# Audio tower on one core: setup moved into the first stage, shift products moved between projection halves, first groups of the last stage shared by VectorE and POOL

## What is computed

```python
# 1: attentive pooling of windows of 4 positions, stride 2 -> 127 patches
A = tanh(x @ W_w.T + W_b + b);  scores = A @ V_w.T + V_b
w = softmax(scores[:, idx]);    h = (w * x[:, idx]).sum(-2) @ P_w.T + P_b
# 2: attention of 8 heads in three parts on a normalized h
h = h + attn(layernorm(h)) @ w_proj.T + b_proj
# 3: four experts, the best one by the router's logits
n = layernorm(h);  e = argmax(n @ router_w + router_b)
h = h + (gelu(n @ w1[e] + b1[e]) @ w2[e] + b2[e] + n)
```

## Time and profile before

| | us |
|---|---|
| median of 3 runs | 1978.07 |
| the profiled execution | 1976.59 |
| its span | 1974.8 |
| setup block | 0 to 30.3 |
| tokenize | 30.6 to 404 |
| attend | 409 to 1492 |
| feed_forward | 1497 to 1975 |
| PE / DVE / ACT / POOL busy | 1814 / 1488 / 1477 / 1263 |

### The profile page before, as it was taken

The page is one execution under the profiler, slowest core; times in us unless marked ns, Lnnn a source line. Parts: engine busy times, 40 slices in busy tenths (PEclk is TensorE's granted clock), DMA queues, the critical chain, the costliest instruction groups (busy, mean ns, idle before and its releaser), DMA issues. The chain is left out here.

```text
span 1974.8 us, 58866 instructions
## 1 busy us (share of the span) xinstructions
PE 1814.1 (92%) x20032; PEld 1012.3 (51%) x20032; DVE 1487.6 (75%) x3655; ACT 1476.9 (75%) x2983; POOL 1262.7 (64%) x2323
## 2 busy tenths in 40 slices
PE   1898889859999999999999999999993999999998
PEld 0566556624444444444444444444442666666666
DVE  3666666768999999999999999999973555555554
ACT  1666666528899999999889989999983666666665
POOL 2666666546777777777777777777744565656551
PEclk9999999969999999999999999999996999999999
DMA  5433433224444444444444444444431222323232
GB/s 142 107 85 90 101 85 99 50 36 81 87 90 88 90 88 88 90 89 89 88 88 89 90 88 90 88 89 88 88 70 27 64 68 63 69 61 69 61 72 49
DMA packets 504063, 159.64 MB, mean 81 GB/s; under 512 B 452176, under 2 KB 503248, under 8 KB 504016
## 3 DMA queue, kind: packets, MB, share of 16 engines
q1 hardware_dynamic: 504016, 159.04, 37.9%
HBM read 37.41 MB, written 12.48 MB: 25 GB/s over the span
## 5 line engine op out<-in xcount | busy, mean ns | idle before, releaser
L726 DVE TENSOR_REDUCE tops<-p_maxa 128x6 f32<-128x762 f32 x512 | 483.1, 944 | 65.1 <-PE p_maxa L568 62.0
L639 PE MATMUL p_o<-probs,vn 127*32 127x256 f32 x6144 | 411.6, 386 | 0.2 <-DVE att L754 0.2
L564 PE MATMUL p_s<-qm,kt 32*128 32x256 f16 x3072 | 401.8, 276 | 2.0 <-DMA qm<-qk 1.0
L680 ACT ACTIVATE probs<-p_s 128x512 f32<-128x512 f32 x512 | 305.6, 597 | 109.1 <-PE p_s L564 95.6
L728 DVE TENSOR_REDUCE tops<-p_maxb 128x4 f32<-128x508 f32 x512 | 346.6, 677 | 0.0
L1000 DVE TENSOR_TENSOR gel_lo<-gel,gel_hi 128x512 f16<-128x512 f32 x192 | 147.1, 766 | 217.4 <-ACT gel_hi L990 216.0
L686 ACT ACTIVATE probs<-p_s 128x512 f32<-128x512 f32 x512 | 308.6, 603 | 0.0
L683 ACT ACTIVATE probs<-p_s 128x512 f32<-128x512 f32 x512 | 304.3, 594 | 0.3 <-PE p_s L564 0.2
L568 PE MATMUL p_maxa<-kt,qt 24*128 24x256 f16 (+1 forms) x2048 | 283.4, 250 | 15.1 <-DMA kt<-qk 8.6
L777 POOL TENSOR_TENSOR qk<-raw,one 128x384 f16<-128x384 f32 x128 | 105.8, 827 | 221.6 <-ACT raw L702 221.6
L982 ACT ACTIVATE gel<-f_w,b 128x512 f32<-128x512 f32 x192 | 131.9, 687 | 144.0 <-PE f_w L933 144.0
(11 more groups left out here) (209 smaller groups left out, 4544.0 us busy)
## 6 DMA issues: line engine op xcount, KB each, us to landing
xt_a<-in_xt SPq DMA_DIRECT2D x32, 512.0 KB, 4.4
xt_b<-in_xt SPq DMA_DIRECT2D x64, 256.0 KB, 5.2
out<-out_sb SPq DMA_DIRECT2D x32, 336.0 KB, 2.7
xt<-hx SPq DMA_TRANSPOSE x128, 2.3
kt<-qk SPq DMA_TRANSPOSE x128, 2.7
qt<-qk SPq DMA_TRANSPOSE x128, 2.5
qm<-qk SPq DMA_TRANSPOSE x128, 2.7
yt<-ay SPq DMA_TRANSPOSE x128, 2.3
```

Of the source, the lines that this page charges most:

```text
L564: return nc.tensor.matmul(o, kt[full(j), r, kind, g, :], qm[full(j), r % 2, versions, g, :], start=True, stop=True, skip_group_check=True)
L639: last = nc.tensor.matmul(p_o[32 * j:32 * j + 32, blocks, :], vn[0:NP, r, src:src + 32], probs[0:NP, r % 2, QUAD * g + j, kind * 256:(kind ...
L680: nc.scalar.activation(probs[:, r % 2, h + 1, 0:512], p_s[1][:, :, :].rearrange("p x n -> p (x n)"), ACT.Exp, scale=SCALE).then_inc(act_e1 ...
L726: nc.vector.tensor_reduce(top[:, q, pair, 4:10], p_ma[:, 0:6, 0:NP], AX.X, ALU.max, negate=True).then_inc(dve_ma[u], 1)
```

## The change

- The setup block is gone. Its loads, VectorE's splits and POOL's matrices are in tokenize. SyncE issues four loads for the first stage's matrices, then the first input, `vw` and `vb`, the second input, and only then the 17 other weights. VectorE makes the first stage's matrices before its loop; the other weights are split in ten portions (`later_weights`), one after each of blocks 2 to 11. TensorE waits for the matrices instead of for a constant.
- In tokenize a projection is made in two halves. The down-shift is between the halves of step 1, the up-shift between those of step 3. VectorE runs softmax step 0 and 1 at steps 1 and 2, behind the band and ahead of the score; step 2 is at step 3, ahead of the band.
- In attend the waits for constants stand at the first use: TensorE's at i = -2, ScalarE's and POOL's at i = -3.
- In feed_forward VectorE makes the high and low halves of the first two groups (`halves`), POOL the rest of them; the fill of `pk` is in three parts and POOL waits only for the part that it needs; SyncE issues the transpose of an input ahead of that of the packed part while i < 0.

The core of the diff:

```diff
@@ tokenize, SyncE @@
+            for dst, src in ((wtf[0][:, :], dram["wt"][0:128, :]), (wtf[1][:, :], dram["wt"][128:256, :]),
+                             (btf[CB:128, :], dram["bt"][CB:128, :]), (tokf[CB:128, :], dram["tok"][CB:128, :])):
+                sp.dma_start(dst, src).then_inc(tok_loaded, 16)
+            load_xt(0, 0)
+            for dst, src in ((t.vw[:, :], dram["vw"]), (t.vb[:, :], dram["vb"])):
+                sp.dma_start(dst, src).then_inc(row_loaded, 16)
+            load_xt(1, 1)
+            for name, parts in splits:
+                for k, w in enumerate(parts):
+                    sp.dma_start(w[:, :], dram[name][128 * k:128 * (k + 1), :]).then_inc(loaded, 16)
...
@@ tokenize, TensorE @@
-            pe.wait_ge(ones, 2)
+            pe.wait_ge(tok_made, 4)
+            pe.wait_ge(built, 3)
...
+                        project(par, k, 0)
-                    if k == 0 and within(i - 1, NG):
+                    if k == 1 and within(i - 1, NG):
 
                         pe.wait_ge(dve_score, seen(i * G))
                         nc.tensor.matmul(p_down, t.below[:, :], score[:, 1 - par, :, 0:2],
                                          start=True, stop=True).then_inc(pe_down, 1)
-                    if k == 2 and within(i - 1, NG):
+                    if k == 3 and within(i - 1, NG):
 
                         pe.wait_ge(dve_weight, seen(i))
                         nc.tensor.matmul(p_up, t.above[:, :], weight[:, 1 - par, :, 2:4],
                                          start=True, stop=True).then_inc(pe_up, 1)
+                    if within(n, NB):
+                        project(par, k, 1).then_inc(pe_a, 1)
...
@@ tokenize, VectorE @@
+                        if k == G - 1:
+                            softmax(i, 1 - par, 2)
                         dve.wait_ge(pool_diag, seen(u + 1))
...
                         last.then_inc(dve_band, 1)
+                    if k in (1, 2):
+                        softmax(i, 1 - par, k - 1)
                     if within(n, NB):
                         dve.wait_ge(act_tanh, seen(n + 1))
...
-                    softmax(i, 1 - par, k)
...
+                    if isinstance(i, int) and 2 <= n < 12:
+                        later_weights(n - 2)
@@ feed_forward, VectorE @@
-            nc.vector.memset(pk[:, :, :, :].rearrange("p r g n -> p (r g n)"), 0.0).then_inc(consts, 1)
+            nc.vector.memset(one[:, :], 1.0)
+            nc.vector.memset(flat(0, 1), 0.0).then_inc(consts, 1)
+            nc.vector.memset(flat(1, 2), 0.0).then_inc(consts, 1)
+
+            def halves(i):
+
+                for k in range(G):
+                    n = (i + 2) * G + k
+                    x = hx[:, i % 2, k, :]
+                    dve.wait_ge(act_ln, n + 1)
+                    nc.vector.tensor_copy(x[:, 0:C], hn[:, k % 2, :]).then_inc(dve_x, 1)
+                    dve.wait_ge(dve_x, 2 * n + 1)
+                    nc.vector.tensor_tensor(x[:, C:2 * C], hn[:, k % 2, :], x[:, 0:C], ALU.subtract).then_inc(dve_x, 1)
+
+            halves(-2)
+            nc.vector.memset(flat(2, U), 0.0).then_inc(consts, 1)
+            halves(-1)
+            dve.wait_ge(consts, 3)
```

More of the change, by code:

```diff
@@ L358, in _, with diagonal @@
         def _(pool):
+            n = 0
+            def diagonal(m, base, value=1.0):
+                nonlocal n
+                nc.gpsimd.memset(m[:, :], 0.0).then_inc(zeroed, 1)
+                n += 1
+                pool.wait_ge(zeroed, n)
+                nc.gpsimd.affine_select(out=m[:, :], in_=m[:, :], compare_op=ALU.not_equal, fill=value, base=base,
+                                        pattern=[[-1, 128]], channel_multiplier=1).then_inc(built, 1)
+            diagonal(t.ident, 0)
+            diagonal(t.below, -1)
+            diagonal(t.above, 1)
+            far = t.split["w1"][3][CB:128, :]
+            pool.wait_ge(built, 3)
+            nc.gpsimd.memset(far, FAR).then_inc(zeroed, 1)
+            n += 1
+            pool.wait_ge(zeroed, n)
+            nc.gpsimd.affine_select(out=far, in_=far, compare_op=ALU.is_ge, fill=0.0, base=0,
+                                    pattern=[[1, NE * HID]], channel_multiplier=-HID).then_inc(zeroed, 1)
+            n += 1
+            pool.wait_ge(zeroed, n)
+            nc.gpsimd.affine_select(out=far, in_=far, compare_op=ALU.is_ge, fill=0.0, base=HID - 1,
+                                    pattern=[[-1, NE * HID]], channel_multiplier=HID).then_inc(built, 1)
+            pool.wait_ge(built, 4)
+            for e in range(NE):
+                nc.gpsimd.memset(t.rank[:, :, e:e + 1], float(NE - e))
             def body(i, par, half):
@@ L550, in _ @@
         def _(pe):
-            pe.wait_ge(consts, 3)
             full = lambda j: slice(32 * j, 32 * j + 32)
@@ L874, in ready, with turn_x @@
                 sp.sem_inc(sp_ready, 1)
+            def turn_x(i, r):
+                if within(i + 2, NG):
+                    ready(pool_x, seen((i + 3) * G))
+                    if isinstance(i, int) and i < 0:
+                        ready(dve_x, (i + 3) * 2 * G)
+                    if isinstance(i, int) and i == -1:
+                        ready(dma_x, 16)
+                    if within(i - 2, NG):
+                        ready(pe_w[HCH - 1], seen(i - 1))
+                    sp.dma_start_transpose(xt[:, (r + 2) % U].rearrange("p g k n -> p (g k) n"),
+                                           hx[:, r % 2].rearrange("p g n -> p (g n)")).then_inc(dma_x, 16)
             def body(i, r, half):
+                if isinstance(i, int) and i < 0:
+                    turn_x(i, r)
                 if within(i - 1, NG):
@@ L1056, in body @@
                     return
+                first = isinstance(i, int) and i < 0
+                if isinstance(i, int) and i <= 0:
+                    pool.wait_ge(consts, i + 3)
                 for k in range(G):
```

205 lines of the change are left out of this document (90 added, 115 removed).

## The result

| | us |
|---|---|
| before, median of 4 | 1978.14 (1976.28 to 1980.55) |
| after, median of 4 | 1944.74 (1944.09 to 1946.12) |
| ratio | 0.9833, 95% interval 0.9821 to 0.9846 |
| span of the profiled execution | 1974.8 before, 1942.9 after |

The change gains 33.4 us by the medians and 31.9 by the two spans. The forecast was 1941, with 1930 to 1947 as the range of its own case and 1928 and 1972 as low and high end. The time lies in both; how the sum came about is another matter, and the larger part of what follows.

A forecast was written before the change was run, and what follows sets the result against it. The first stage was taken as bound by its setup prelude, then a ring through all engines (11.29 us a cycle). Gains 23.7 + 6.7 + .6 + 4.8 = 35.8 off 1976.59 gave 1941; low end 1928, high end 1972.

The forecast's parts named there:

- (a): Setup moved into the first stage: first projection matmul at 13.0 instead of 40.56, 27.5 us less.
- (b): Later weights split over ten blocks of the first stage: 3.8 us lost, bounds 1.5 and 8.
- (c): Shift products between projection halves in the first stage: cycle 11.05 instead of 11.29, 6.7 us gained over 28 cycles.
- (d): Waits for constants moved in the attention stage: .6 us gained, bounds 0 and .7.
- (e): First groups of the last stage, halves shared with VectorE: 4.8 us gained, bounds 2.5 and 7.5.
- The port is lost: First stage: POOL's next lo beats `weight` to the shared port, cycle 12.15, 31 us more, 1972 in all; chance .16.
- the race: First stage: `weight` against POOL's next lo for the shared port, forecast to be won with .06 us in hand.
- slower: First stage: TensorE's clock falls after the pause, .16 more per matmul; nothing gained, or 1995 with twelve; chance .03.
- TensorE bound: First stage: cycle falls to 9.7, TensorE's work alone, 38 us more gained, 1903 in all; chance .08.
- the ring: First stage: a chain of dependences through all engines sets the cycle, 11.29 us before and 11.05 after.

The follow-up runs named there:

- late_casts: Changed kernel with the later weights' casts and subtractions in the last ten blocks of the first stage's last three groups, not blocks 2 to 11: 1945.65 us.
- spread: Changed kernel with negated maximum in PSUM, softmax ahead of the band at steps 1 and 2, later weights' casts one to a block from block 7: 1900.30 us.
- psum_least: Changed kernel with the negated maximum of the scores in PSUM instead of SBUF: 1940.52 us, ratio .9815 to the kernel before.
- pool_halves: Changed kernel with POOL again making the halves of the last stage's first two groups, the shorter clearing kept: 1949.87 us, ratio .9869 to the kernel before.
- undo_last: Changed kernel with the last stage of the kernel before: 1954.60 us, ratio .9888 to the kernel before.
- h_first: Changed kernel with ScalarE's copy h of step 1 ahead of the exponential instead of behind it: 2005.60 us, ratio 1.0151 to the kernel before.
- ahead: Changed kernel with the softmax at steps 1 and 2 ahead of the band on VectorE: 1904.18 us, ratio .9623 to the kernel before.

## Why the prediction was right, and where it was not

By its own steps:

(a) *First matmul.* Forecast 13.0, measured 13.55: 27.0 gained instead of 27.5. ScalarE starts at 10.33 instead of 9.9, the matmul 3.22 behind it instead of 3.07. The method (issues, landing, the way through the engines) held.

(b) *The later weights.* The term that was mis-sized: 3.8 forecast, 7.2 measured (27.0 at the first matmul, 19.8 left by the fifth down-shift: 92.66 before, 74.36 after, and 1.46 for its later place in the cycle), inside its bounds of 1.5 and 8. The last load was forecast near 24 and is there at 23.43; VectorE stands 2.00, not 3.4. What was left out are three things. The third input is queued on SyncE behind those loads (3.69 on ScalarE). TensorE's clock falls to .50 for 3.4 us at 26.9, behind its wait of 1.89 for a score at the first down-shift; it is busy throughout, so this costs up to 1.7, an estimate from half the busy time. And later instructions meet POOL at the port, on either side: the first cast takes 1.25 behind a lo, the last difference, of one row, 1.21, and POOL's diag 1.61 behind the largest difference:

```profile
48.68 1.42 DVE L273 TENSOR_TENSOR w_lo<-w2f,w_hi 128x1152 f16<-128x1152 f32 x1
...
48.96 1.61 POOL L381 TENSOR_TENSOR diag<-ident,weight 128x256 f32<-128x256 f32 x1
```

late_casts shows VectorE's work to be what holds these groups, the clock's fall included (5.2 back by the fourth down-shift); spread shows the input right behind it.

(c) *The cycle.* Forecast 11.05 by a ring that ends at the up-shift with a wait of 1.3; measured 11.13, with a wait of 1.37 at ph of step 2 and none at the up-shift. The number was nearly right and the path wrong. Up to `shifted` every step is as forecast (lo of step 1 first at the port by .15, `shifted` 1.03 for .97). The step that failed is the next: in working out the lost port I listed ScalarE's queue behind the exponential, h among it, and never asked who waits for h. TensorE does, at ph of step 2, 1.5 ahead of the up-shift. That the wait found there, 1.37, is as long as the one forecast, 1.3, is chance. That the cycle came out near 11.05 is less so: `weight` starts 3.01 behind lo of step 1, forecast 2.95 to 2.97, so the two paths are almost equally long, and the up-shift could not have come much before 192.11 in any case. psum_least, which takes .86 out of the one, finds the other: .46 at the up-shift. The cycle gave 4.0 us over the stage where 6.7 were forecast.

(d) *Attention.* First product at 390.06, 24.37 earlier where the first stage ended 23.84 earlier: .5, as forecast (.6). Over the whole stage nothing of it is left, +.07: the changed kernel's profile has the stretch of 3.4 us at .50 told above, with TensorE busy throughout, and the profile before has none. Half of it, 1.7 by estimate, is more than the .5; that this is where the .5 went is not shown.

(e) *Last stage.* 8.1 instead of 4.8, beyond the upper bound of 7.5; the second term mis-sized. The block was taken as 1.35 or 1.0 and is .92. So VectorE is through with its second group 12.8 after the attention's end, where the forecast had 15.5 (1508.3), and the choice, forecast at 1.9 and there in 1.9, is not held by it. The failing step is that VectorE's and POOL's times were added. In the rows, VectorE's difference takes .63 instead of the .34 of the same size without POOL, but it spends the excess while POOL's f_res runs at its usual .60; only f_pk gets longer, .40 for .29. The two engines take turns, and what waits is the one that would be idle anyway. The second group gained 2.6 more where I had .6 (the wait for its input, .56): the other 2.0 is TensorE's clock, which the sum left out, by the busy times at .50 under pool_halves (8.1 against 4.1, half the difference). Of the 9.0, .9 is given back behind it. With undo_last and pool_halves the gain divides into 5.9 with VectorE's share, .5 for the fill, and 1.7 up to the second group; by the estimate the clock is .8 of the first and 1.2 of the last.

In sum: 27.0 - 7.2 + 4.0 for the first stage, .5 - .6 for the attention and 8.1 for the last, 31.8 (the spans differ by 31.9), where the forecast had 27.5 - 3.8 + 6.7 + .6 + 4.8 = 35.8. Two misses of 3.4 and 3.3 in opposite senses and one of 2.7 made an error of 3.9 in the profile and 3.7 in the median. The sum was better than its terms.

**The rivals.** *The port is lost* did not happen, and the race was not the one described: since ph of step 2 is late, so are z, split and lo (192.58), and `weight` at 191.79 has .8 in hand, not .06. h_first shows that the rival was real and close: move one copy on ScalarE and it comes, at 13.49 rather than 12.15. The *slower* rival is there too, in the same run: it priced a pause of 2.4 and .16 for each slow matmul, and h_first shows a pause of 2.15 and ten such matmuls, 1.7 of its cycle. So the two are nearly one case: 23 of the 26 cycles that lost the port lost the clock too, and 1972 should have been some 2005. In the three others the port alone makes 11.8, where 12.15 was priced. *TensorE bound*, at 9.7, was given .08 on the ground that the ring gave 11.29 to a hundredth. That tested nothing: its parts are distances between rows of that same cycle (5.35 is from the up-shift at 211.55 to the next down-shift), so they had to add up to it. And ahead shows that the ring could be cut with one move: 9.63. A ring that fits tells what the time is, not how firmly it is held.

The Trainium skill (SBUF — State Buffer, Who interferes with whom) adds to what the prediction took from it that an instruction of VectorE with at most one SBUF input, outside the modes that use both ports, does not contend with POOL, while one with two does. The runs here agree: `weight` beside a lo already under way takes 1.05 with two and .17 with one. It also says that a cast can enter such a mode and then contend. That agrees as well: the first cast of the later weights takes 1.25 beside POOL's lo (23.24 to 24.39), and .42 in spread, where it starts ahead of one. What the prediction made of that, 1.35 for a block and 3.7 gained in the last stage, does not follow: in these rows contention lengthens VectorE's instructions and POOL's f_pk, while f_res, which holds the port, keeps its .60.

## What to carry to other kernels

When an instruction gets later, list all that stands behind it in its own engine's queue, and for each of these ask who waits for it; the bill may come from there, as here from a copy behind an exponential. Put short links of a long chain ahead of an instruction that waits for another engine, not behind it: that was worth 37.7 us in the first stage, and the shift between the halves 4 to 7. And before work is moved under other work, look whether a second, equally late thing hides beneath: TensorE showed no wait for the input behind the weights until the casts were gone. And price TensorE's clock as a term of its own: by the estimates above it is 2.0 us of the last stage's gain, and 1.7 a cycle of h_first.

## What the runs showed of the hardware

- With one operand in PSUM a VectorE addition of 16 columns no longer waits for POOL: 1032 ns become 171.
- The holder of the port can be VectorE as well: the diag of 1.61 above, and in the last stage an f_res of POOL of .98 instead of .60 beside a fill and a cast of VectorE.
- A wait of 1.21 of TensorE in each cycle of 11.00 leaves the granted clock at 1.00; of 26 waits of 2.15 in h_first, 23 are followed by 3.4 us at .50 (cycle 13.49) and three are not (11.8).
- Behind the attention TensorE's clock is at .50 for some time: it is back at 1.00 some 22 us after the attention's end in the changed kernel, 30 in pool_halves and 33 before and in undo_last, 4.1, 5.8 and 8.7 us behind the first expert product in the first three.
- The attention stage, the same code each time, took 1084.4 to 1088.9: 1086.2 to 1088.9 where one more stretch of 3.4 us at .50 falls into it, 1084.4 to 1086.5 where none does. The kernel before has none and took 1088.21. What brings such a stretch about was not looked into.
